# A four-layer convolution kernel: the order of ScalarE's and VectorE's work in the neighbour layer, and the loading of the residual in the sweep layer, are changed

## The reference

```python
cn = xc / jnp.maximum(jnp.linalg.norm(xc, axis=1, keepdims=True), EPS_NORM)
sim = jnp.einsum('bcp,bckp->bkp', cn, pn)
...
out = jnp.einsum('bckp,bkp->bcp', pat_sorted, wts).reshape(B, C, H, W)
enhanced = out + _group_norm(x, gn_weight, gn_bias)
h = jax.nn.relu(jnp.einsum('oi,bihw->bohw', w1, enhanced) + b1[None, :, None, None])
ffn = jnp.einsum('oi,bihw->bohw', w2, h) + b2[None, :, None, None]
return enhanced + ffn
```

## Time and profile before

| | us |
|---|---|
| median of 3 runs | 6378.55 (6375.53 to 6380.76) |
| profiled execution | 6372.76 |
| its span in the trace | 6371.0 |
| PE busy | 5211.8 (82%) |
| DVE busy | 4159.3 (65%) |
| ACT busy | 2407.6 (38%) |
| POOL busy | 2260.0 (35%) |

### The profile page before, as it was taken

One profiled execution on the slowest core, in us unless ns is written; L12 is line 12 of the kernel. 1 busy time (PEld: TensorE's weight loads), 2 busy tenths in 40 slices (PEclk: granted clock), 3 DMA queues, 4 the chain that ended last, 5 costly groups with the idle time before them and its releaser, 6 DMA issues. The chain is left out here.

```text
span 6371.0 us, 127916 instructions
## 1 busy us (share of the span) xinstructions
PE 5211.8 (82%) x49134; PEld 4132.8 (65%) x49134; DVE 4159.3 (65%) x7316; ACT 2407.6 (38%) x4304; POOL 2260.0 (35%) x1348
## 2 busy tenths in 40 slices
PE   2878787878787878165858569999979999999996
PEld 1656565656565555043535347777779999999996
DVE  5767676777777767676666659999733333455564
ACT  1656666666566656222323236565410000000000
POOL 1535354545454545322323238888700000000020
PEclk9989898988888989576878789999989999999998
DMA  3000000000000000332323120111040000000034
GB/s 135 15 28 15 28 17 27 28 15 28 28 17 27 20 24 10 101 105 67 119 71 114 54 76 29 37 46 49 23 148 0 0 0 0 0 0 0 0 53 132
DMA packets 224343, 268.75 MB, mean 42 GB/s; under 512 B 157728, under 2 KB 159008, under 8 KB 216736
## 3 DMA queue, kind: packets, MB, share of 16 engines
q1 hardware_dynamic: 92576, 246.10, 11.1%
q10 hardware_dynamic: 131328, 16.78, 1.7%
HBM read 156.27 MB, written 67.11 MB: 35 GB/s over the span
## 5 line engine op out<-in xcount | busy, mean ns | idle before, releaser
L2359 DVE SCALAR_TENSOR_TENSOR l_state<-l_conv,l_state 128x256 f32 (+1 forms) x500 | 292.3, 585 | 787.3 <-PE l_conv L2290 787.3
L527 POOL TENSOR_TENSOR l_probs<-l_probs,l_inv 128x1024 f32<-128x1024 f32 x256 | 493.0, 1931 | 567.9 <-DVE l_inv L937 567.3
L2290 PE MATMUL l_conv<-l_carry_hi,l_taps_hi 128*128 128x248 f32 (+2 forms) x4500 | 626.5, 284 | 35.0 <-DVE l_carry_hi L2344 35.0
L2290 PE MATMUL l_conv<-l_carry_lo,l_taps_hi 128*128 128x248 f32 (+2 forms) x4500 | 621.6, 283 | 6.0 <-DVE l_carry_lo L2346 6.0
L2290 PE MATMUL l_conv<-l_carry_hi,l_taps_lo 128*128 128x248 f32 (+2 forms) x4500 | 626.4, 284 | 0.0
L2290 PEld LDWEIGHTS l_conv<-l_carry_hi,l_taps_hi 128*128 128x128 f32 x4500 | 578.5, 190 | 38.3 <-DVE l_carry_hi L2344 38.2
L2145 DVE SCALAR_TENSOR_TENSOR l_acc<-l_xpad,l_w,l_acc 128x1024 f32<-128x1024 f32 x448 | 574.5, 1289 | 14.8 <-ACT l_acc L2046 1.3
L2290 PEld LDWEIGHTS l_conv<-l_carry_hi,l_taps_lo 128*128 128x128 f32 x4500 | 579.7, 190 | 0.0
L2290 PEld LDWEIGHTS l_conv<-l_carry_lo,l_taps_hi 128*128 128x128 f32 x4500 | 575.3, 189 | 6.9 <-DVE l_carry_lo L2346 6.9
L1965 POOL TENSOR_TENSOR l_sum<-l_sum,l_prod 128x1024 f32<-128x1024 f32 x224 | 539.1, 2407 | 111.1 <-ACT l_prod L2062 92.6
L606 PEld LDWEIGHTS l_upper<-l_rows_T,l_hats 128*64 128x64 f32 x16384 | 516.7, 142 | 86.5 <-issue 84.7
(11 more groups left out here) (295 smaller groups left out, 9491.4 us busy)
## 6 DMA issues: line engine op xcount, KB each, us to landing
l_xleft<-l_xt SPq DMA_DIRECT2D x64, 283.5 KB
l_xright<-l_xt SPq DMA_DIRECT2D x64, 283.5 KB
stat_xs<-in_x SPq DMA_DIRECT2D x8, 2048.0 KB, 23.5
l_hats<-in_x SPq DMA_DIRECT2D x8, 2048.0 KB, 7.9
l_xraw<-in_x SPq DMA_DIRECT2D x8, 2048.0 KB, 8.7
after_layer<-l_xraw SPq DMA_DIRECT2D x64, 256.0 KB, 2.0
l_xblk<-after_layer SPq DMA_DIRECT2D x32, 512.0 KB, 5.2
l_xsum<-after_layer SPq DMA_DIRECT2D x32, 512.0 KB, 5.6
```

What stands on the lines that cost most here:

```text
L527: pool.tensor_tensor(part, part, inv[:, u, cols].rearrange("c (j o) -> c j o", o=1).to_broadcast([C, 4, KEYS]), ALU.mult).then_inc(scaled_ ...
L2290: last = pe.matmul(conv[h][:, 0:HB * W].rearrange("c (b w) -> c b w", b=HB)[:, :, lo:lo + ncol], w[:, s, k, :], carry[:, h, :, at:at + nco ...
L2359: dve.scalar_tensor_tensor(row, conv[h][:, 0:HB * W].rearrange("c (b w) -> c b w", b=HB), 0.0, row, op0=ALU.max, op1=ALU.add).then_inc(lin ...
```

## The change

Neighbour layer: on ACT, `square` of block c-1 moves from behind `relu 1` to the place between `enhance` and `norm`. On DVE, `build` 3 and 4 move ahead of `side_prods`, 5 and 6 ahead of `side_sums`, 7 to 9 ahead of `pool_sums`, which is now behind all ten matrices. No instruction is added or removed there.

Sweep layer: the residual is loaded in three parts: right halves as before (8 DMAs of 1024 KB), then the second quarters of the width (8 of 512 KB), then the first quarters (8 of 512 KB). The quarters have a buffer for each image, in the same memory as the four halves. POOL adds the right halves as before and then the second quarters ("middle"), 128x1024 each, once three quarters of the last sweep are done; DVE adds the first quarters, one operation of 128x1024 an image. SP's stores wait for all three.

```diff
--- before.py
+++ after.py
@@ -1591,6 +1591,8 @@
                         put_stage(t, c, u)
                     if before:
                         enhance(*block_before(t, c, 1), 1 - u)
+                    if t < PAIRS and not (isinstance(c, int) and c == 0):
+                        square(t, c - 1)
                     if t < PAIRS:
                         norm(t, c, u)
                     if before:
@@ -1600,8 +1602,6 @@
                     if before:
                         copy_ffn(g, 1 - u, 0)
                         relu(g, 1)
-                    if t < PAIRS and not (isinstance(c, int) and c == 0):
-                        square(t, c - 1)
                     if before:
                         copy_ffn(g, 1 - u, 1)
                 steps(act, t, step)
@@ -1776,19 +1776,17 @@
                 def step(c, u):
                     lagging = t < PAIRS and not (isinstance(c, int) and c == 0)
                     if t >= 1:
-                        build(t, c, 0, 1, 2)
+                        build(t, c, 0, 1, 2, 3, 4)
                     if lagging:
                         side_prods(t, c - 1, 1 - u)
                     if t >= 1:
-                        build(t, c, 3, 4)
+                        build(t, c, 5, 6)
                     if lagging:
                         side_sums(t, c - 1)
                     if t >= 1:
-                        build(t, c, 5, 6)
+                        build(t, c, 7, 8, 9)
                     if lagging:
                         pool_sums(t, c - 1)
-                    if t >= 1:
-                        build(t, c, 7, 8, 9)
                     if second_before(t, c):
                         stats(*block_before(t, c, 2), u)
                 steps(dve, t, step)
...
         carry_lo = mem.sbuf("carry_lo", [C, HALVES, HB, EDGE + W + EDGE], FP32R)
-        SLOTS, MID = 4, W // 2
-        xres = mem.sbuf("xres", [C, SLOTS, H, MID])
-        wraws = [xres[:, :, :, :].rearrange("c s h w -> c (s h w)")[:, s * C * K:(s + 1) * C * K].rearrange("c (i k) -> c i k", k=K)
-                 for s in range(4)]
+        SLOTS, MID, QUARTER = 4, W // 2, W // 4
+        xres = mem.sbuf("xres", [C, SLOTS * H * MID])
+        wraws = [xres[:, s * C * K:(s + 1) * C * K].rearrange("c (i k) -> c i k", k=K) for s in range(4)]
+        halves = [xres[:, s * H * MID:(s + 1) * H * MID].rearrange("c (h w) -> c h w", w=MID) for s in range(SLOTS)]
+        quarters = [xres[:, b * H * QUARTER:(b + 1) * H * QUARTER].rearrange("c (h w) -> c h w", w=QUARTER) for b in range(B)]
...
-        def residual(p):
-
-            return x_in[p % B].rearrange("c (h w) -> c h w", w=W)[:, :, MID * (p < B):MID * (p < B) + MID]
+        def residual(b, lo, hi):
+
+            return x_in[b].rearrange("c (h w) -> c h w", w=W)[:, :, lo:hi]
...
             for b in range(B):
                 for part in range(2):
                     sp.wait_ge(right_added, b + 1)
-                    sp.wait_ge(left_added, 2 * b + part + 1)
+                    sp.wait_ge(middle_added, b + 1)
+                    sp.wait_ge(left_added, b + 1)
                     sp.dma_start(out[b][:, part * (HW // 2):(part + 1) * (HW // 2)],
...
-            for p in range(2 * B):
-                if SLOTS <= p < B + SLOTS:
-                    act.wait_ge(right_added, p + 1 - SLOTS)
-                elif p >= B + SLOTS:
-                    act.wait_ge(left_added, 2 * (p + 1 - SLOTS - B))
-                act.dma_start(xres[:, p % SLOTS, :, :], residual(p)).then_inc(res_loaded[p % SLOTS], 16)
+            for b in range(B):
+                wait(act, right_added, b + 1 - SLOTS)
+                act.dma_start(halves[b % SLOTS], residual(b, MID, W)).then_inc(half_loaded[b % SLOTS], 16)
+            for b in range(B):
+                act.wait_ge(right_added, b // 2 + SLOTS + 1)
+                act.dma_start(quarters[b], residual(b, QUARTER, MID)).then_inc(quarter_loaded[b], 16)
+            for b in range(B):
+                act.wait_ge(middle_added, b + 1)
+                act.dma_start(quarters[b], residual(b, 0, QUARTER)).then_inc(quarter_loaded[b], 16)
...
         def _(pool):
             for b in range(B):
 
                 pool.wait_ge(lo_ready[b // HB], BEFORE[3] + (W - 2 - MID) + 2)
-                pool.wait_ge(res_loaded[b % SLOTS], 16 * (b // SLOTS + 1))
-                half = state[:, b, :, MID:W]
-                pool.tensor_tensor(half, half, xres[:, b % SLOTS, :, :], ALU.add).then_inc(right_added, 1)
+                pool.wait_ge(half_loaded[b % SLOTS], 16 * (b // SLOTS + 1))
+                right = state[:, b, :, MID:W]
+                pool.tensor_tensor(right, right, halves[b % SLOTS], ALU.add).then_inc(right_added, 1)
+            for b in range(B):
+
+                pool.wait_ge(lo_ready[b // HB], BEFORE[3] + (W - 2 - QUARTER) + 2)
+                pool.wait_ge(quarter_loaded[b], 16)
+                middle = state[:, b, :, QUARTER:MID]
+                pool.tensor_tensor(middle, middle, quarters[b], ALU.add).then_inc(middle_added, 1)
...
-            def add_left(*pieces):
-
-                for q in pieces:
-                    b, r = q // 2, q % 2 * (H // 2)
-                    dve.wait_ge(res_loaded[b % SLOTS], 16 * ((B + b) // SLOTS + 1))
-                    half = state[:, b, r:r + H // 2, 0:MID]
-                    dve.tensor_tensor(half, half, xres[:, b % SLOTS, r:r + H // 2, :], ALU.add).then_inc(left_added, 1)
+            def add_left(b):
+
+                dve.wait_ge(quarter_loaded[b], 32)
+                left = state[:, b, :, 0:QUARTER]
+                dve.tensor_tensor(left, left, quarters[b], ALU.add).then_inc(left_added, 1)
...
                         if q < HB:
-                            add_left(2 * q, 2 * q + 1)
+                            add_left(q)
...
             dve.wait_ge(lo_ready[1], BEFORE[3] + STEPS[3] + 1)
-            add_left(*range(2 * HB, 2 * B))
+            for b in range(HB, B):
+                add_left(b)
...
```

More of the change, by code:

```diff
@@ L2218, in layer3 @@
         waits_met = mem.sem("waits_met")
-        res_loaded = [mem.sem(f"res_loaded{k}") for k in range(SLOTS)]
+        half_loaded = [mem.sem(f"half_loaded{k}") for k in range(SLOTS)]
+        quarter_loaded = [mem.sem(f"quarter_loaded{b}") for b in range(B)]
         right_added = mem.sem("right_added")
+        middle_added = mem.sem("middle_added")
         left_added = mem.sem("left_added")
```

## The result

| | before | after |
|---|---|---|
| median of 4 runs, us | 6379.66 (6375.53 to 6383.16) | 6199.23 (6193.73 to 6204.46) |
| profiled execution | 6372.76 | 6202.02 |
| its span | 6371.0 | 6200.1 |
| PE busy | 5211.8 (82%) | 5117.1 (83%) |
| DVE busy | 4159.3 (65%) | 4151.1 (67%) |

The ratio of the medians is 0.9717, its 95% interval 0.9700 to 0.9734: 180 us faster, where 176.5 was forecast.

The account below looks back on a forecast made before the run. PE waits and loses clock because DVE's matrices stand behind sums held by ACT's late square; the end waits for residual loads. -173 + 17 - 21.5 + 1 = -176.5 us, median 6202 us, range 6184 to 6262 (its own 6184 to 6232).

Parts of the forecast that it names:

- Stages 1 to 3: Neighbour layer: with square and matrices early, steps of 21.0 us and 156 us a stage, -173 us over three stages.
- rival 1: Neighbour layer: DVE is the bound, POOL's operations block it until a step is 24 us; 6256 us, chance 0.14.
- quick step: Neighbour layer, kernel before: a step said to have its matrices in time, 20.55 us at clock 1.00.
- The 28.0 us: Neighbour layer: upper end for a step, 17.5 + 10.5, if each POOL operation blocks DVE once in full.
- Rival 2: Neighbour layer: PE has its matrices but not the clock, steps of 27.2 us, +112, 6314 us; chance 0.07.
- Rival 3: Neighbour layer: stage 0's loop binds stages 1 to 3 too, steps of 32 us, slower at 6424 us; chance 0.03.
- rival 4: Neighbour layer: pool_sums still waits for POOL's late products, so the step is not freed; 6375 us, chance 0.02.
- Stage 4: Neighbour layer: no sums there, so its steps of 18.6 us at clock 1.00 stay; no change.
- Stage 0: Neighbour layer: norm now stands behind the square, 28.2 us for two blocks instead of 22.9; +17 us.
- The end: Sweep layer: stores no longer share the DMA engines with loads, 40.6 us of transfer; -21.5 us.
- The middle adds: Sweep layer: POOL's eight new adds of 2.3 us hold up DVE's splits, +0.5 per train, +1 us.
- The sum: Whole kernel: -176.5 us against 6372.76 gives 6196 for the profiled execution, 6202 for the median.

Follow-up runs that it names:

- e3: Changed kernel, but in stage 0 alone ACT squares in the old place, behind relu 1; 6183.23 us, ratio 0.9688 to the kernel before.
- e4: Changed kernel with POOL's right adds of 128x2048 each done as two of 128x1024; 6186.33 us, ratio 0.9695 to the kernel before.
- e6: Kernel before with the neighbour layer's part of the change alone; 6216.13 us, ratio 0.9754 to the kernel before.
- e7: Changed kernel with stage 0's old place of the square and right adds in two pieces; 6169.36 us, ratio 0.9680 to the kernel before.
- e8: Changed kernel with stage 0's old place of the square and all POOL's adds cut to 128x512; 6155.29 us, ratio 0.9661 to the kernel before.
- e1: Changed kernel with DVE's old order of matrices in the neighbour layer, the square still early; 6207.45 us, ratio 0.9730 to the kernel before.
- e2: Changed kernel with the square back behind relu 1 in all stages, DVE's new order kept; 6199.30 us, ratio 0.9717 to the kernel before.
- e5: Kernel before with the sweep layer's part of the change alone; 6351.52 us, ratio 0.9966 to the kernel before.

## Why the prediction was right

**Stages 1 to 3: -169 against -173.** The mechanism was the one told: no wait for the square, the matrices in time but for one step, PE at its high clock. Inside the windows of the earlier trace rows the three stages take 159.61 + 154.70 + 154.66 = 469.0 us, where 3 x 156 = 468 was forecast. Steps are 20.6 us, under the 21.0 I took; the part after the start on block 7 takes 31 us, not 30; and in stage 1 one step took 25.8 us, as its timeline shows:

```profile
2815.99 7.09 DVE L1636 TENSOR_TENSOR l_wdiag<-l_diag,l_wsrc 128x192 f32<-128x192 f32 x5
...
2818.60 0.89 PE L1466 MATMUL l_gather_ps<-l_wdiag,l_stage 64*128 64x64 f32 x12 [1.73 <-DVE l_wdiag L1636]
2821.13 1.65 PE L1466 MATMUL l_gather_ps<-l_wdiag,l_stage 64*128 64x128 f32 x12 [1.64 <-DVE l_wdiag L1636]
```

Five matrices beside POOL's two products took 7.09 us where I counted 3.9, and PE waited for them twice. That is rival 1's mechanism, once in 18 steps and not in every one; e3 and e4 have the same step of 25.8 us, e6, e7 and e8 don't. The 3 us that are missing otherwise lie outside those windows, between the end of the sums and block 1 of stages 2 and 3 (76.8 and 78.7 us, before 76.1 in both), where I had counted nothing.

**The quick step was misread.** The length of a step was forecast from the window 3045.55 to 3066.10 of the kernel before, as "20.55 us at clock 1.00", "which had its matrices in time". That window isn't a step. It holds 114 matmuls, and a step has 150. The rest comes behind it, after PE waited for a matrix there too, and PE's next start is 26.36 us after the last one (timeline of the kernel before):

```profile
3066.47 3.19 PE L1466 MATMUL l_gather_ps<-l_wdiag,l_stage 64*128 64x192 f32 x24 [2.75 <-DVE l_wdiag L1636]
...
3071.91 3.06 PE L1453 MATMUL l_gather_ps<-l_xsum,l_gdiag 128*128 128x512 f32 x4
```

No step of stages 1 to 3 of the kernel before was shorter than 26.3 us from block 1 on. That the measured 20.60 fell on the 20.55 is luck in this reading. Other rows do give it: 18.6 us of a step of stage 4, and in the kernel before 0.60 and 0.66 us for the two halves of `turn` with a wait of 0.83 between them, 20.7 together. Some busy times on DVE were too long as well: matrices 7 to 9 take 1.48 us and not 2.2, so that of their 5.52 us 4.0 were blocked and not 3.3. And the steps and ends from which the range was added up (20.55 and 28.5, 22 and +10) give 6189 to 6229, not 6184 to 6232.

**Rival 1** (steps of 24 us) fell with the steps of 20.60, but not by much: DVE is busy 20.46 us of them. Its 17.5 us of work grew by 3 us of blocks, close to the 3.3 before, and not by POOL's whole 12.58. The sums go on beside POOL, and only the products and matrices pay. The 28.0 us, all of POOL's time added to DVE's, counts the sums as held too, so waiting for whole operations of POOL does not lead to it. **Rival 2** (PE without its clock) fell with clock 0.97 to 0.98. **Rival 3** (stage 0's loop binds later stages too, steps of 32 us) and **rival 4** (the step isn't freed) fell with steps of 20.6 us. What the forecast did not see is that either move alone would have done: it argued from both, and e1 and e2 show 147 us of gain that either has (152 + 164 - 169).

**Stage 4: -2.8 against 0.** The steps stayed at 18.65 us, as forecast. The difference is the stage's first step, 20.4 us against 23.1. It took 20.3 to 22.8 us in the other runs with both moves, and why was not looked into.

**Stage 0: +17.3 against +17.** Three times in the stage two blocks take 28.1 to 29.3 us (the pair shown above 17.8 and 11.4) instead of 22.9; I had worked out 28.2.

**The end: -22.9 against -21.5.** The stores took 39.8 us, where I took 40.6. Their rate is between 364 and 466 GB/s in every full slice, in most above 400. The page "DMA: Bandwidth & Descriptors" of the Trainium skill (section "Where 436 GB/s comes from") gives about 358 GB/s for HBM on a core, as half of a figure for two cores. This kernel runs on one; these rows go above it, and the 46.9 us that follow from it did not come.

**The middle adds: the term that was mis-sized.** The sentence "I take +0.5 per train, **+1**" measured 1.45 a train, 2.9 in all. The first train in the changed kernel:

```profile
6054.43 10.18 POOL L2340 TENSOR_TENSOR l_state<-l_state,l_xres 128x1024 f32<-128x1024 f32 x4 [67.66 <-DVE l_carry_lo L2357]
...
6059.77 0.74 DVE L2370 SCALAR_TENSOR_TENSOR l_state<-l_conv,l_state 128x256 f32 x1
...
6062.36 2.63 DVE L2357 TENSOR_TENSOR l_carry_lo<-l_state,l_carry_hi 128x256 fp32r<-128x256 f32 x1
6064.91 0.71 DVE L2370 SCALAR_TENSOR_TENSOR l_state<-l_conv,l_state 128x256 f32 x1
```

An add is 2.55 us, not 2.3, so a line needs 5.1 us. The four lines from the train's start are 4.21, 5.14, 1.91 and 3.15 us: two long ones, and one short one that catches up. The other 3.5 us of the sweep's +6.4 were not in the forecast. About 1.9 of them follow the first right train, where two lines took 2.59 and 4.38 us and before 1.91 and 3.15. They are this one profile's: in the four variants with the changed sweep layer and whole right adds (e1, e2, e3, e5) the same two lines took 1.90 and 3.2 us, and the sweep 1666.0 to 1668.6. With the old sweep layer it took 1665.6 (before) and 1663.3 (e6), so the change costs the sweep about 3 us, which is the middle trains' 2.9; the rest of the 6.4 is scatter.

**The sum** came out 5.7 us short against the profiled execution (6202.02 against 6196), from 4 in the stages and 5.4 in the sweep, less 2.8 in stage 4 and 1.4 at the end. That the median came within 3 us of the 6202 is chance in part: the profiled execution of before lies 7 us under its median, that of after 3 us over.

## What to carry to other kernels

When two engines hold each other through one late operation, look for every place where the chain can be cut: here the first cut took nearly all of the gain, and each further one must be judged by itself, stage by stage, since the same reordering that frees the full stages can cost a stage that has only half of the work. An order of work that the code writes once for all stages may be wrong for the first and the last. And when POOL works beside DVE on data in SBUF, cut its operations until two of them fit into the period of the loop they disturb: POOL then needs more time and the kernel less.

## What the runs showed of the hardware

- A DVE operation that copies or combines data in SBUF waits for the POOL operation in progress, and then gets its turn between two of POOL's even when these stand back to back: the second part of a split took 4.73 us beside adds of 4.6, 2.60 beside adds of 2.5, and 1.51 to 1.53 beside adds of 1.4. L2370, with its operand from PSUM, is not held: 0.71 to 0.78 us beside the changed kernel's adds, 0.75 away from them. Nor are DVE's sums, as two rows of the step of stage 2 show, in which they start in the middle of a product of POOL's and take 1.21 us and 1.2 each, as they do alone:

```profile
3077.56 2.87 POOL L1399 TENSOR_TENSOR l_prod<-l_xt,l_xright 128x1024 f32<-128x1024 f32 x1
...
3078.14 1.21 DVE L1680 TENSOR_REDUCE l_inv_avg<-l_xt  x1
...
3079.27 2.33 DVE L1676 TENSOR_REDUCE l_dots<-l_prod 128x1024 f32 x2
```

- The other way round POOL did not get a turn between DVE's operations. This addition of POOL's, 1.27 us alone, started while DVE ran matrices, side products and matrices back to back, and ended 1.2 us after the start of DVE's first sum (L1680 at 3137.37; changed kernel, stage 2). Three additions of the stages 1 to 3 took 5.1 to 6.5 us in this way:

```profile
3132.14 6.45 POOL L1407 TENSOR_TENSOR l_res<-l_res,l_enh 128x512 f32<-128x512 f32 x1 [3.02 <-ACT l_res L1556]
```

- Cutting POOL's adds costs POOL little: the data of one image's right half took 4.64 us in one operation, 5.05 in two and 5.67 in four (18.56, 20.19 and 22.69 us for four images).
- With DVE busy 99% of a step (20.46 of 20.60 us), PE and its weight loads waited only 3.4 and 20.1 us for matrices in four stages. A full engine was no bound here, with what is due early first in its order.
- Stores alone from one core ran at 400 to 466 GB/s in most slices, 16.78 MB in 39.8 us.
